# Depthwise convolution as banded matmuls: four windows of one image side by side in 384 columns, channels on the array's row groups

## The reference, cut to what matters

```python
B, C, H, W = 2, 64, 96, 96
h = group_norm1(x, n1_g, n1_b)                  # one mean and variance for a whole image
f = dwconv(h, w3, b3) + dwconv(h, w5, b5) + dwconv(h, w7, b7)     # depthwise, zero padding
g = sigmoid(conv1x1(f, gate_w, gate_b))
x = x + conv1x1(f * g, proj_w, proj_b)
h = group_norm1(x, n2_g, n2_b)
q, k, v = conv1x1 of h with q_w, k_w, v_w       # each N = 9216 pixels x 64 channels
attn = softmax(q @ k * C ** -0.5)               # 9216 x 9216 for each image
out = x + attn @ v
```

## Time and profile before

| what | us |
|---|---|
| median of three executions | 2980.9 |
| profiled execution, whole | 2982.3 |
| its span in the trace | 2980.6 |
| TensorE busy with matmuls | 2831.4 |
| VectorE busy | 2506.4 |
| ScalarE busy | 2258.7 |
| GpSimd busy | 1767.1 |

### The profile page before, as it was taken

One profiled execution on the slowest core, in us unless ns is written; L12 is line 12 of the kernel. 1 busy time (PEld: TensorE's weight loads), 2 busy tenths in 40 slices (PEclk: granted clock), 3 DMA queues, 4 the chain that ended last, 5 costly groups with the idle time before them and its releaser, 6 DMA issues.

```text
span 2980.6 us, 57612 instructions
## 1 busy us (share of the span) xinstructions
PE 2831.4 (95%) x21297; PEld 971.8 (33%) x21297; DVE 2506.4 (84%) x3038; ACT 2258.7 (76%) x2362; POOL 1767.1 (59%) x1436
## 2 busy tenths in 40 slices
PE   6657999999999999999998899999999999999998
PEld 3433333333333333333332333333333333333332
DVE  4137999999999999999956899999999999999984
ACT  5016788888888888888886678888888888888887
POOL 1013566666666666666665466666666666666666
PEclk9878999999999999999998999999999999999999
DMA  4222010000000000000001000000000000000000
GB/s 125 59 56 65 13 37 10 10 10 10 10 10 10 10 10 10 10 10 10 8 5 43 8 8 10 10 10 10 10 10 10 10 10 10 10 10 10 11 11 4
DMA packets 47715, 53.11 MB, mean 18 GB/s; under 512 B 19776, under 2 KB 45888, under 8 KB 46928
## 3 DMA queue, kind: packets, MB, share of 16 engines
q1 hardware_dynamic: 47440, 49.46, 6.9%
HBM read 21.12 MB, written 14.16 MB: 12 GB/s over the span
## 4 chain that ended last, share of the span: by engine, by line
PE 85%; DVE 8%; issue 4%; ACT 2%; DMA 0%; SPq 0%; POOL 0%; POOLq 0%; DVEq 0%; ACTq 0%
PE ps L921 37%; PE ps L912 31%; PE ps L928 11%; DVE mxp L734 4%; PE ps L1034 2%; PE ps L1011 1%; DVE arena L757 1%; DVE ps L747 1%; ACT arena L504 1%; PE ps L944 1%; DVE ps L750 0%; ACT rsum L521 0%; DVE bn L825 0%; DVE arena L835 0%; DVE x_max L826 0%
## 5 line engine op out<-in xcount | busy, mean ns | idle before, releaser
L440 POOL TENSOR_TENSOR arena<-arena 128x512 f32<-128x512 f32 x1224 | 1556.8, 1272 | 810.5 <-ACT arena L504 730.5
L734 DVE TENSOR_REDUCE mxp<-ps 128x1 f32<-128x1024 f32 x1296 | 1571.3, 1216 | 207.2 <-PE ps L928 206.1
L504 ACT ACTIVATE arena<-ps,bnd 128x1024 f32<-128x1024 f32 x1296 | 1373.0, 1110 | 415.6 <-PE ps L912 345.0
L921 PE MATMUL ps<-arena 128*64 128x512 f32 x5184 | 1268.4, 605 | 1.0 <-ACT pvb L514 1.0
L912 PE MATMUL ps<-arena 64*128 64x512 f16 x7776 | 1058.0, 378 | 11.5 <-ACT rsum L521 5.9
L750 DVE TENSOR_TENSOR ps<-ps,arena 128x512 f32<-128x512 f32 x1260 | 868.9, 690 | 74.8 <-ACT arena L504 74.8
L542 ACT ACTIVATE ps<-mseed 128x1024 f32<-128x1024 f32 x612 | 629.1, 1028 | 57.1 <-ACT arena L504 1.5
L928 PE MATMUL ps<-arena,QM 64*128 64x512 f16 x2592 | 501.4, 383 | 18.4 <-DVE mxp L734 10.2
L912 PEld LDWEIGHTS ps<-arena 64*128 64x128 f16 x7776 | 372.7, 94 | 440.6 <-issue 33.2
L921 PEld LDWEIGHTS ps<-arena 128*64 128x64 f32 x5184 | 311.0, 136 | 510.7 <-issue 354.8
L928 PEld LDWEIGHTS ps<-arena,QM 64*128 64x128 f16 x2592 | 125.2, 93 | 731.9 <-DVE mxp L734 625.2
(11 more groups left out here) (114 smaller groups left out, 761.0 us busy)
## 6 DMA issues: line engine op xcount, KB each, us to landing
arena<-arena SPq DMA_DIRECT2D x144, 64.0 KB, 2.0
arena<-in_x_rows SPq DMA_DIRECT2D x8, 816.0 KB, 10.2
xs<-in_x SPq DMA_DIRECT2D x4, 1152.0 KB, 14.4
f_scratch<-arena SPq DMA_DIRECT2D x32, 144.0 KB
f<-f_scratch SPq DMA_DIRECT2D x64, 72.0 KB
x_scratch<-arena SPq DMA_DIRECT2D x4, 1152.0 KB, 13.9
QM<-arena SPq DMA_DIRECT2D x72, 64.0 KB, 2.0
xst<-x_scratch SPq DMA_DIRECT2D x72, 64.0 KB, 2.2
```

The lines of the kernel that those rows point to most:

```text
L440: nc.gpsimd.tensor_tensor(accA[:, n % 2, :], accA[:, n % 2, :], e, ALU.add).then_inc(adda_free, 1)
L504: nc.scalar.activation(flat(E[:, slot_of(n % 2, p), :, :]), flat(ps[:, S_BANK + 2 * buf:S_BANK + 2 * buf + 2, :]), ACT.Exp, scale=bnd[:, 6 ...
L734: nc.vector.reduce_max(flat(mxp[:])[:, v:v + 1], flat(ps[:, bank:bank + 2, :]), AX.X).then_inc(mx_free, 1)
L921: a = nc.tensor.matmul(ps[C * t:C * t + C, ACC_BANK, :], V[:, t, p, :], E[:, slot_of(par, p), t, :], start=(p == 0), stop=(p == NPAIR - 1) ...
```

## The change

A matmul of the convolution now takes one channel of one image with its four windows side by side: 4 x 96 = 384 columns. The row groups of the array hold four channels and the column groups four more, so a set is 16 channels of one image: 112 matmuls, 4 sets an image, 8 in all. Image 0 is convolved first, and image 1's statistics are made between its second and third set. Gamma and beta are now applied to the rows, with one ScalarE instruction per 4 channels (16 an image), since they differ between row groups; the halo rows outside of the image are then set to zero on VectorE (image 0) and on GpSimd (image 1). Bands are built by 96 matmuls of 112 columns into six PSUM banks and taken out by six ScalarE copies of 448 columns. The 1x1 matrices arrive transposed from the host. Pixels have another order inside a channel (row in window, window, column), and the host undoes it on the output. Everything from the gate on is as before, apart from the number and shape of the transfers that bring the convolved data in.

```diff
-COLS = 4
-CSET = 2 * COLS
-NSET = C // CSET
-BAND_ROWS = 3
+GROUPS, COLS = 4, 4
+NK = C // GROUPS
+NSET = NK // COLS
+WN = WINDOWS * W
+TAP_COLS = NK * KW
+BAND_ROWS = 4
-        arena = sb("arena", [P, N_XR + N_BANDS])
+        arena = sb("arena", [P, N_E + 2 * N_Q + NHALF])
 # SyncE
-                    sp.dma_start(f_dram[s, k].rearrange("(g r) k b x -> r g (k b x)", g=WINDOWS),
-                                 evac[GRP * k:GRP * k + WROWS, s % 2, :, :]).then_inc(f_out[s % 2], 16)
+                    sp.dma_start(f_dram[b, c:c + GROUPS, :].rearrange("g (r n) -> r g n", r=WROWS),
+                                 evac[GRP * h:GRP * h + WROWS, s % 2, :, :]).then_inc(f_out[s % 2], 16)
-                        sp.dma_start(f[c:c + COLS, :].rearrange("c (y x) -> c y x", x=W),
-                                     f_dram[s, :, HR * half:HR * half + HR, k, b, :]).then_inc(f_in, 16)
+                    sp.dma_start(f[C * half:C * half + C, :][at, :], f_dram[b, at, half * NHALF:(half + 1) * NHALF]
+                                 ).then_inc(f_in, 16)
...
-            sp.wait_ge(bands_out, BAND_GROUPS)
-            sp.wait_ge(wt_ready, 1)
+            sp.wait_ge(bands_ps, BAND_GROUPS)
             sp.wait_ge(wstat_ready, 1)
 # GpSimd
+            for k in range(NSET):
+                for e, w in enumerate((0, WINDOWS - 1)):
+                    pool.wait_ge(rows_scaled, NK + COLS * (k + 1))
+                    at = xr[:, 1, COLS * k:COLS * k + COLS, w, PAD:PAD + W]
+                    nc.gpsimd.tensor_tensor(at, at, edges[:, e:e + 1].unsqueeze(2).to_broadcast([P, COLS, W]), ALU.mult
+                                            ).then_inc(xr_ready, 1)
 # ScalarE
-                at = xr[:, b, CSET * s:CSET * s + CSET, PAD:PAD + W]
-                nc.scalar.activation(at, at, ACT.Identity, bias=aff1[:, 2 * b + 1:2 * b + 2], scale=aff1[:, 2 * b:2 * b + 1]
-                                     ).then_inc(xr_ready, 1)
+                at = xr[:, b, k, :, PAD:PAD + W]
+                nc.scalar.activation(at, at, ACT.Identity, bias=aff1[:, b, 1, k:k + 1], scale=aff1[:, b, 0, k:k + 1]
+                                     ).then_inc(rows_scaled, 1)
 # VectorE
+            def mask_rows(k):
+                dve.wait_ge(rows_scaled, COLS * (k + 1))
+                for e, w in enumerate((0, WINDOWS - 1)):
+                    at = xr[:, 0, COLS * k:COLS * k + COLS, w, PAD:PAD + W]
+                    nc.vector.tensor_scalar(at, at, edges[:, e:e + 1], None, ALU.mult).then_inc(xr_ready, 1)
...
             joint_kernel()
+            dve.wait_ge(const_ready, 4)
+            row_masks()
             row_stats(0)
+            row_norm(0)
+            for k in range(NSET):
+                mask_rows(k)
+            row_stats(1)
+            take_convolved(0)
+            row_norm(1)
+            nc.vector.tensor_copy(ident16[:], ident[:]).then_inc(const_ready, 1)
             weight_norms()
-            row_stats(1)
-            for s in range(NSET):
+            for s in range(1, 2 * NSET):
                 take_convolved(s)
 # TensorE
+            for i in range(BAND_GROUPS):
+                for k in range(BAND_ROWS):
+                    for g in range(GROUPS):
+                        a = nc.tensor.matmul(ps[GRP * g:GRP * g + GRP, i, k * TAP_COLS:(k + 1) * TAP_COLS],
+                                             shifts[0:K_ROWS, BAND_ROWS * i + k, :], wsum[0:K_ROWS, g * TAP_COLS:(g + 1) * TAP_COLS],
+                                             start=True, stop=True, tile_position=(0, GRP * g))
+                a.then_inc(bands_ps, 1)
...
+                for dx in range(KW):
+                    for g in range(GROUPS):
+                        rows = slice(GRP * g, GRP * g + GRP)
+                        for h in range(COLS):
+                            k = COLS * q + h
+                            a = nc.tensor.matmul(
+                                ps[GRP * h:GRP * h + WROWS, 4 * (s % 2) + g, 0:WN].rearrange("p (w x) -> p w x", x=W),
+                                bands[rows, k * KW + dx, :], xr[rows, b, k, :, dx:dx + W],
+                                start=(dx == 0), stop=(dx == KW - 1), tile_position=(GRP * g, GRP * h))
                 a.then_inc(conv_ps, 1)
-            for s in range(NSET):
-                convolve(s)
-            pe.wait_ge(conv_out, NSET)
+            convolve(0, 0)
+            convolve(0, 1)
+            pe.wait_ge(conv_out, 1)
+            stats(2, core, STAT1_BANK[1])
+            pe.wait_ge(var_ready, 2)
+            convolve(0, 2)
+            convolve(0, 3)
+            for q in range(NSET):
+                convolve(1, q)
+            pe.wait_ge(conv_out, 2 * NSET)
```

More of the change, by code:

```diff
@@ L163, in program @@
         x_ready = sem("x_ready")
-        xr_in = [[sem(f"xr_in{b}{q}") for q in range(QUARTERS)] for b in range(B)]
+        xr_in = [[sem(f"xr_in{b}{q}") for q in range(NSET)] for b in range(B)]
         cw_in = sem("cw_in")
@@ L315, in _ @@
             load_x(0)
-            sp.wait_ge(bands_out, BAND_GROUPS)
-            sp.wait_ge(wt_ready, 1)
+            sp.wait_ge(bands_ps, BAND_GROUPS)
             sp.wait_ge(wstat_ready, 1)
-            for s in range(NSET):
[L320 to L324, removed]
+            for q in range(NSET):
+                put_convolved(0, q)
+                if q:
+                    written(q - 1)
+                    get_convolved(0, q - 1)
@@ L325, in _ @@
+            written(NSET - 1)
             get_convolved(0, NSET - 1)
+            for q in range(NSET):
+                put_convolved(1, q)
             def stage_queries(at, half):
@@ L391, in _ @@
                     sp.wait_ge(v_ps, NCH * (b + 1))
-                    for s in range(NSET):
-                        get_convolved(b + 1, s)
+                    written(2 * NSET - 2)
+                    written(2 * NSET - 1)
+                    for q in range(NSET):
+                        get_convolved(b + 1, q)
                 with sp.Fori(1, NCH - 1) as ii:
@@ new lines, in row_stats, with row_norm @@
+            def row_stats(b):
+                for k in range(NK):
+                    if k % COLS == 0:
+                        dve.wait_ge(xr_in[b][k // COLS], 16)
+                    nc.vector.bn_stats(bn1[:, k, :], xr[:, b, k, :, PAD:PAD + W]).then_inc(bn1_done, 1)
+                dve.wait_ge(bn1_done, NK * (b + 1))
+                nc.vector.bn_aggr(mv[:], flat(bn1[:])).then_inc(st_in, 1)
+            def row_norm(b):
+                dve.wait_ge(rowp_in, 16)
+                moments(b, 1.0 / H)
+                nc.vector.tensor_scalar(tot[:, 0:1], tot[:, 0:1], -1.0, None, ALU.mult)
+                chain(nc.vector.tensor_scalar(aff1[:, b, 0, :], rowp[:, 0, :], tot[:, 1:2], None, ALU.mult))
+                nc.vector.scalar_tensor_tensor(out=aff1[:, b, 1, :], in0=aff1[:, b, 0, :], scalar=tot[:, 0:1],
+                                               in1=rowp[:, 1, :], op0=ALU.mult, op1=ALU.add).then_inc(aff_ready, 1)
@@ L998, in attend @@
                     weigh(par, p + 1, n0 + p + 1)
[L1000 removed]
+            pe.wait_ge(shifts_ready, 1)
             pe.wait_ge(wsum_ready, 1)
[L1002 to L1016 removed]
@@ L1019, in _, with convolve @@
+            for bank in (BAND_GROUPS, BAND_GROUPS + 1):
+                nc.tensor.matmul(ps[:, bank, 0:GROUPS * TAP_COLS], shifts[0:K_ROWS, 0:P // GRP, :].rearrange("p r i -> p (r i)"),
+                                 wsum[0:K_ROWS, :], start=True, stop=True)
+            pe.wait_ge(core_ready, 1)
+            stats(0, core, STAT1_BANK[0])
             pe.wait_ge(bands_out, BAND_GROUPS)
-            pe.wait_ge(wt_ready, 1)
-            pe.wait_ge(aff_ready, 2)
-            def convolve(s):
-                pe.wait_ge(xr_ready, NSET + s + 1)
+            def convolve(b, q):
+                s = NSET * b + q
+                pe.wait_ge(xr_ready, 2 * (s + 1))
@@ L1026, in convolve @@
                 if s >= 2:
                     pe.wait_ge(conv_out, s - 1)
-                for k in (0, 1):
-                    for dx in range(KW):
-                        for g in range(WINDOWS):
-                            rows = slice(GRP * g, GRP * g + GRP)
-                            for h in range(COLS):
-                                c = CSET * s + COLS * k + h
-                                a = nc.tensor.matmul(
-                                    ps[GRP * h:GRP * h + WROWS, 4 * (s % 2) + g, k * B * W:(k + 1) * B * W].rearrange(
-                                        "p (b x) -> p b x", b=B),
-                                    bands[rows, c * KW + dx, :], xr[rows, :, c, dx:dx + W],
-                                    start=(dx == 0), stop=(dx == KW - 1), tile_position=(GRP * g, GRP * h))
@@ L1129 @@
     columns = [np.tile(raw[n], 2)[:, None] for n in both]
-    rows = np.zeros((B, P, C, XW), np.float32)
-    for g in range(WINDOWS):
-        first = max(0, WROWS * g - PAD)
-        last = min(H, WROWS * g - PAD + WIN)
```

(18 more changed lines are left out.)

251 lines of the change are left out of this document (101 added, 150 removed).

## The result

The changed kernel takes 2881.52 us (median of four, 2878.6 to 2882.61) against 2981.03 us for the kernel before, measured beside it: ratio 0.9668, 95% interval 0.9651 to 0.9685. Forecast were 2870 us and a range of 2857 to 2893. So 99.5 us were gained where about 111 were forecast. The profiled execution took 2882.6 us, 99.7 less than the one before, with a span of 2880.9.

The account below looks back on a forecast made before the run. Attention was taken as TensorE-bound, convolution as bound by instruction packets. First matmul 26, convolution 60, copy and step 1.9 put the gate at 87.9 instead of 197.3; with 1.5 from the gate's clock, 2870 us, range 2857 to 2893.

Parts of the forecast that it names:

- Bound by instruction packets: Convolution: TensorE waits for its instructions, not its columns; 28 packets of 256 at 3.84 us each make the 107.6 us.
- rival (3): Convolution: columns or row groups decide, the stage keeps its 107.6 us; median 2922 us, chance 0.04.
- Convolution 60 us: Convolution stage: 14 packets, taken as 54 us, plus 2 for half clock, 3.5 for the pause, 0.5 for fetches.
- rival (1): Convolution: the clock falls in pauses and stays low, a packet costs up to 6.5 us; 2900 to 2907 us, chance 0.10.
- A burst of 3.6 us at full clock, 6.2 at the half clock: Convolution: doubling the columns lengthens a 128-matmul burst from 2.29 to 3.6 us, or 3.61 to 6.2 at half clock.
- The pause, 3.5 us: Convolution, before set 2: TensorE waits for image 1's statistics, about 3.5 to 5 us, with 3.5 in the sum.
- Preparation, first matmul at 26: Before the convolution: cheaper bands and an earlier start put its first matmul at 26 us (22 to 32) instead of 70.72.
- Tail and gate: After the convolution: read back hidden, 1.9 us of copy and step instead of 18.9; first gate matmuls about 1.5 us less.
- Attention: Attention after the gate: same operations at other buffer addresses, taken as 0 change, bounds -5 and +5 us.
- rival (5): Attention: VectorE's reads and additions get dearer at new addresses and become the bound; at 14%, 3020 us; chance 0.02.
- Rival (4): Before the gate: VectorE's order chains image 1 behind image 0, TensorE idle 20 us more; 2890 us, chance 0.04.
- Rival (2): Convolution: no fetch limit, fetch runs ahead at 3.3 us a packet, stage 46 us; 2862 us, chance 0.06.

Follow-up runs that it names:

- the two repeats: The changed kernel, unaltered, run twice more as a measure for the variants: 2882.37 us (ratio 0.9663) and 2880.66 us (0.9659).
- experiment 8: Changed kernel with the early start of image 0 undone: TensorE convolves only once image 1's statistics and both images' first sets are ready; 2908.06 us (0.9751).
- experiment 7: Changed kernel without scratch for image 0, channels copied straight into the gate's tile: 2894.87 us (0.9708); with ScalarE issuing half the transfers, 2895.78 us (0.9706).
- experiment 2: Changed kernel with image 0's reads from the scratch issued only after the last write of image 1: 2896.6 us (0.9707).

## Why the prediction was right, point by point

- *Bound by instruction packets.* Shown by two things together. Halving the columns left the pace: 107.4 us for 28 packets at 96 columns and 107.6 at 192, and periods of 3.7 to 4.1 us at 384. And the holes grew when fewer packets came through beside the reads (4 for 7 in the same 26 us). At 384 columns and the full clock the burst is 3.6 us of that period, so columns and fetch are nearly level there. One sign of being wrong did show, two packet periods of 7.4 and 9.05 us (55.60 to 63.01, 69.48 to 78.53), but the reads made them and not the columns. The rule that fetching is mostly hidden (Trainium skill, "Runtime: NRT & Kernel Launch", Instruction fetch mechanics) does not hold for this stage, and rival (3), which followed from it, is out.
- *Convolution 60 us.* The mechanism was right and one term was mis-sized: "0.5 us for fetches behind the denser scratch traffic" was short by about 11 (11.4 by 72.1 against 60.7 with the reads away; 8.7 to 11.4 with the two repeats): it left out what the reads, eight of 288 KB issued as soon as their data lay in the scratch, do to the packets. Two holes of 3.79 and 5.38 us where 0.4 is usual make 8.4, and the first burst behind, 5.96 for 3.6, 2.4 more. Of rival (1), the half clock behind a long hole, this is the mild form. And that the rest comes to 60.7 is in part luck. By 3.84 us a packet, 14 packets are 53.8; with the reads away the first 149 matmul instructions took 3.7 us more than their share (the working had 2), the pause 1.9 (3.5), and sets 2 to 7 1.5 more (0.5). The 2 us stood for the half clock, but the granted clock reads 1.00 in that stretch, with the transfer engines full (share 1.02 from 24 to 28 us); what slowed it was not tested. The clock fell behind the pause instead, to 0.59 from 44 to 48 us.
- *A burst of 3.6 us at full clock, 6.2 at the half clock.* Measured 3.61 and 5.96, the latter at a granted clock of 0.53. The full-clock number rested on 1.3 us of columns inside the 2.29 us burst, which the 96-column run does not bear out: the sum was right by luck, its parts not. The rows have the same 3.61 us for 192 columns at the half clock and 3.6 for 384 at the full clock.
- *The pause, 3.5 us.* Measured from the end of the burst at 42.86 to 44.71, 1.9 us, since the first two sets took 17 us and not 15.
- *Preparation, first matmul at 26.* 25.81. Bands 9.18 us from 5.87, statistics from 7.43; factors from the first small matmul in 4 us, not 5.5; and the two warming matmuls, 3.28 us that I had not counted, put the statistics matmul 2.8 us behind VectorE's result.
- *Tail and gate.* 1.8 us as forecast, the gate 1.0 for 1.5 us.
- *Attention.* Unchanged but for 1.2 us in all that follows; rival (5) is out. Rival (4) too: TensorE's idle time for image 1 is the pause alone. Rival (2) is out: at 384 columns packets come 3.7 to 4.1 us apart in a quiet stretch. Its price was unsound too: 3.3 us a packet is less than the burst of 3.6 us that the same working expects, so that without any limit by the fetch the stage would have been 14 x 3.6 = 50 us and not 46.

## What to carry to other kernels

Count instructions against their packets before counting columns: where the bursts between holes hold the same number of instructions each time, larger instructions are the cure (here half as many, with the same columns in sum), down to the point where a burst is as long as the fetch. Such a stage is then exposed to every transfer on the same engines: keep few bytes queued (two small reads under way at a time cost TensorE about 1 us here, 62.0 against 60.7, and eight large ones at will 9 to 11). And start on the part of the data that is complete: starting on one image gave 26 us here.

## What the runs showed of the hardware that I had not expected

- GpSimd's masks began 7.2 to 8.1 us after its all-reduce had begun, in the changed kernel, its two repeats and eight of the variants, though the record of the all-reduce is 0.39 us long and the rows of the first four instructions had been ready for over 5 us (in the changed kernel at about 49 us). Two timeline lines of the changed kernel:

```profile
47.25 0.39 POOL L443 PARTITION_ALL_REDUCE wmax<-wstat  x1 [40.85 <-DVE wstat L684]
54.61 6.34 POOL L450 TENSOR_TENSOR arena<-arena,edges 128x384 f32<-128x384 f32 x8 [6.97 <-ACT arena L585]
```

  Between the two stand two MODIFY_POOL_CONFIG instructions of GpSimd, at 47.6 us in the changed kernel; whether they are the reason was not tested. With both images awaited (experiment 8) the gap stood in the chain: first rows ready at 47.6 us, masks from 53.38, 5.8 us of the 9 above.
- The transfers of experiment 7, each of which ends in two partitions, moved 50 GB/s together, from one issuing engine or two, where the reads of experiment 2, issued last, moved 2.36 MB in about 21 us, some 110 GB/s.
